# Flamingo gated cross-attention with a mixture of experts: the residual moved from VectorE to ScalarE and GpSimd, its bias to TensorE, prelude and last batch in another order

## The reference

```python
# attention, per batch
q = layernorm(x) @ wq + bq ; k = ctx @ wk + bk ; v = ctx @ wv + bv      # 16 heads
score = (q k^T) / sqrt(16) * mask
score = where(score == 0, -1e9, score)
heads = softmax(score) v  @ wo + bo
x = x + tanh(g_xattn) * heads
# experts, per token
probs = softmax(layernorm(x) @ router_w + router_b); top 2, renormalized -> gates
x = x + tanh(g_ffn) * sum_e gates_e * (silu(xn @ w1_e) * (xn @ w3_e)) @ w2_e
```

## Time and profile before

| | |
|---|---|
| three runs, median (lowest to highest) | 487.54 us (487.33 to 488.08) |
| profiled execution | 488.64 us |
| its span in the trace | 486.7 us |
| PE busy | 460.7 us, 95% |
| PEld busy | 433.4 us, 89% |
| DVE busy | 378.6 us, 78% |
| ACT busy | 307.0 us, 63% |
| POOL busy | 196.0 us, 40% |

### The profile page before, as it was taken

The page is one execution under the profiler, slowest core; times in us unless marked ns, Lnnn a source line. Parts: engine busy times, 40 slices in busy tenths (PEclk is TensorE's granted clock), DMA queues, the critical chain, the costliest instruction groups (busy, mean ns, idle before and its releaser), DMA issues.

```text
span 486.7 us, 11552 instructions
## 1 busy us (share of the span) xinstructions
PE 460.7 (95%) x3720; PEld 433.4 (89%) x3720; DVE 378.6 (78%) x876; ACT 307.0 (63%) x768; POOL 196.0 (40%) x204
## 2 busy tenths in 40 slices
PE   7899899989869999999999999999999999999995
PEld 5578797877767999899999999999999999999894
DVE  1577998978964888886888888888878878878772
ACT  2426555464435667686767767777767767776782
POOL 4428686597784045342146253113303303302312
PEclk9989999999979999999999999999999999999999
DMA  8619998842113104032023132122112102102112
GB/s 256 162 42 392 380 410 312 335 179 90 39 50 112 47 22 90 12 80 24 23 31 70 38 66 45 24 44 26 33 33 44 21 22 33 22 13 34 23 13 23
DMA packets 33968, 45.22 MB, mean 93 GB/s; under 512 B 10183, under 2 KB 30613, under 8 KB 33685
## 3 DMA queue, kind: packets, MB, share of 16 engines
q1 hardware_dynamic: 25999, 35.21, 21.6%
q0 software_dynamic: 6576, 8.92, 10.9%
q10 hardware_dynamic: 1344, 0.48, 0.5%
HBM read 32.91 MB, written 21.82 MB: 112 GB/s over the span
## 4 chain that ended last, share of the span: by engine, by line
PE 68%; DVE 16%; ACT 5%; issue 4%; POOL 3%; ACTq 1%; DMA 1%; DVEq 0%; SPq 0%; POOLq 0%
PE ps_rows L1764 22%; PE ps_wide L1784 7%; PE ps_probT L1764 7%; PE ps_misc L1784 7%; PE ps_wide L1593 5%; DVE w_lo L1404 3%; PE ps_misc L1615 2%; PE ps_misc L1547 2%; PE ps_rows L1813 2%; DVE w_lo L1400 2%; PE ps_probT L1573 2%; PE ps_wide L1824 1%; PE ps_rows L1561 1%; DVE score L1314 1%; DVE ps_rows L1409 1%
## 5 line engine op out<-in xcount | busy, mean ns | idle before, releaser
L1227 POOL DMA_INDIRECT out_x<-y_out,meta x35 | 64.0, 1830 | 190.9 <-ACT y_out L1026 185.8
L1404 DVE TENSOR_TENSOR w_lo<-w,w_hi 128x512 fp32r<-128x512 f32 x152 | 104.1, 685 | 13.4 <-issue 6.6
L1764 PE MATMUL ps_rows<-xt_hi,w_hi 128*128 128x256 f32 x384 | 110.6, 288 | 0.2 <-DVE xt_lo L1418 0.2
L1764 PE MATMUL ps_rows<-xt_hi,w_lo 128*128 128x256 f32 x384 | 108.6, 283 | 0.0
L1764 PE MATMUL ps_rows<-xt_lo,w_hi 128*128 128x256 f32 x384 | 108.6, 283 | 0.0
L975 ACT CAST w_hi<-w 128x512 fp32r x152 | 95.2, 627 | 4.2 <-issue 3.9
L1764 PEld LDWEIGHTS ps_rows<-xt_hi,w_hi 128*128 128x128 f32 x384 | 73.6, 192 | 0.4 <-DVE xt_lo L1418 0.4
L1764 PEld LDWEIGHTS ps_rows<-xt_lo,w_hi 128*128 128x128 f32 x384 | 73.6, 192 | 0.0
L1764 PEld LDWEIGHTS ps_rows<-xt_hi,w_lo 128*128 128x128 f32 x384 | 73.5, 192 | 0.0
L989 ACT ACTIVATE act_g<-ps_rows 128x256 f32<-128x256 f32 x96 | 37.3, 389 | 28.7 <-PE ps_rows L1764 24.0
L1004 ACT CAST hid_hi<-ps_rows 128x256 fp32r<-128x256 f32 x96 | 36.1, 376 | 27.1 <-DVE ps_rows L1409 26.3
(11 more groups left out here) (241 smaller groups left out, 1160.9 us busy)
## 6 DMA issues: line engine op xcount, KB each, us to landing
grouped<-in_pad SPq DMA_DIRECT2D x1, 10296.0 KB
w<-in_L_ffn_w SPq DMA_DIRECT2D x8, 1024.0 KB, 12.2
w2s<-in_L_ffn_w SPq DMA_DIRECT2D x4, 1024.0 KB, 13.7
xg<-grouped SPq DMA_DIRECT2D x16, 256.0 KB, 2.7
out_x<-xall SPq DMA_DIRECT2D x8, 256.0 KB, 7.0
xall<-in_x SPq DMA_DIRECT2D x1, 1024.0 KB, 12.6
xall<-in_x SPq DMA_DIRECT2D x1, 768.0 KB, 7.9
ctxT<-in_ctx_t SPq DMA_DIRECT2D x2, 308.0 KB, 5.4
```

The costliest lines, as they stand in the source:

```text
L1227: pool.indirect_dma_start(out, bass.IndirectOffsetOnAxis(ap=meta[:, s % 2, t, E:E + 1].bitcast(U32), axis=0), y_out[:, s % 2, t, :], None, ...
L1404: dve.tensor_tensor(w_lo[:, f % NB], unit_weights(e, f), w_hi[:, f % NB].bitcast(F32), ALU.subtract).then_inc(w_lo_done, 1)
L1764: mm = pe.matmul(ps_gu[f % NB][:, m, 0:n], lhs, rhs[:, a, c, 0:n], start=(k == 0), stop=(k % (3 * DC) == 3 * DC - 1), skip_group_check=True)
```

## The change

1. **Residual.** For batches 0 to 5 VectorE's fused add goes from `body`. ScalarE's new `gain_copy(b-1)` copies `ps_misc * tanh_g` into a new SBUF buffer `gain` at the end of its body b, and GpSimd's new `add_gain(b-1)` adds that to `xall` at the end of its body b, behind `keys(b+1, 1)`. Batches 6 and 7 keep VectorE's add. `turn_x` and `turn_ctx` now wait for ScalarE's copy (`attended_out`).
2. **Bias.** GpSimd's eight `bias_add` go. `bos` is no longer scaled, and `project_o` begins with a product of one row: ones times `bos`, over both tiles, 512 columns.
3. **Prelude.** The last four strips of `vblock` are issued by GpSimd instead of ScalarE, ahead of its body 0, on a semaphore of their own. ScalarE's `norm(1)` and `xT_copy(1)` move out of body 0 to between its copies of the values. TensorE does `turn_x(1)` and `project_q(1)` earlier; `values(3)` goes to the bank `ps_probT` in place of `ps_misc`.
4. **Last batch.** GpSimd's `context(6, 1)` goes ahead of `deviation2`. VectorE's slot counts of group 0 leave body 6, but for a first one, for steps 1 and 3 of body 7.

The core of the diff:

```diff
-        ps_vals = [ps_probT, ps_route, ps_wide, ps_misc]
+        ps_vals = [ps_probT, ps_route, ps_wide, ps_probT]
...
-                place_values(sp, 0, STRIPS[:-BY_ACT])
-                place_values(sp, 1, STRIPS)
+                place_values(sp, 0, STRIPS[:-BY_POOL], ld_vblock[0])
+                place_values(sp, 1, STRIPS, ld_vblock[1])
...
                 def q_copy(b):
                     act.wait_ge(q_done, b + 1)
+                    if b:
+                        act.wait_ge(scores_done, RG * DC * b)
...
+                def gain_copy(b):
+                    act.wait_ge(wo_done, b + 1)
+                    if b == 0:
+                        act.wait_ge(tanh_done, 1)
+                    else:
+                        act.wait_ge(x2_done, b)
+                    act.activation(gain[:].rearrange("p t d -> p (t d)"), ps_misc[:], ACT.Copy, scale=tanh_g[:, 0:1]).then_inc(attended_out, 1)
...
-                            act.wait_ge(tanh_done, 1)
-                            act.activation(bos, ps_misc[:, 0:D], ACT.Copy, scale=tanh_g[:, 0:1]).then_inc(bo_ready, 1)
+                            act.copy(bos, ps_misc[:, 0:D]).then_inc(bo_ready, 1)
...
                         probT_exp(b, 2, first)
+                    if not first:
+                        gain_copy(b - 1)
...
                 q_copy(0)
+                norm(1)
                 vals_copy(2)
                 vals_copy(3)
-                place_values(act, 0, STRIPS[-BY_ACT:])
+                xT_copy(1)
...
-                def bias_add(b):
-
-                    pool.wait_ge(norm_done, 2 * b + 2)
-                    pool.tensor_tensor(xall[:, bass.ds(b * QT, QT), :], xall[:, bass.ds(b * QT, QT), :], wide(bos, QT),
-                                       ALU.add).then_inc(biased, 1)
+                def add_gain(b):
+
+                    pool.wait_ge(attended_out, b + 1)
+                    pool.tensor_tensor(xall[:, bass.ds(b * QT, QT), :], xall[:, bass.ds(b * QT, QT), :], gain[:], ALU.add).then_inc(x2_done, 1)
...
-                    if b in BEGIN:
+                    if b in BEGIN and not last:
                         deviation2(pool, BEGIN[b])
...
                         context(pool, b - 1, 1)
+                    if last:
+                        deviation2(pool, BEGIN[b])
...
                         keys(b + 1, 1)
-                    if first:
-                        pool.wait_ge(bo_ready, 1)
-                        bias_add(b)
-                        bias_add(b + 1)
+                    if not first and not last:
+                        add_gain(b - 1)
...
                 keys(0, 1)
+                place_values(pool, 0, STRIPS[-BY_POOL:], ld_vblock_end)
...
-                    dve.wait_ge(biased, b + 1)
+                    dve.wait_ge(x2_done, b)
...
                         if s == 0 and b > 1:
-                            residual(b - 2)
                             batch_stats(dve, b - 2)
                         if (b, s) == (B - 2, 0):
+                            hand_out_count(dve, 0)
+                        if (b, s) == (B - 1, 1):
                             hand_out(dve, 0)
-                        if (b, s) == (B - 2, 1):
+                        if (b, s) == (B - 1, 3):
                             hand_out_begin(dve, 0)
                             hand_out_owner(dve, 0)
-                        if (b, s) == (B - 1, 1):
                             hand_out_rest(dve, 0)
...
-                        pe.wait_ge(x2_done, b - 2)
+                        pe.wait_ge(attended_out, b - 2)
...
                     pe.wait_ge(ctxT_copied, b + 1)
+                    pe.matmul(ps_misc[:].rearrange("p (t d) -> p t d", t=QT), one_row[0:1, :], wide(bos[0:1, :], QT),
+                              start=True, stop=False, skip_group_check=True)
...
                 scores(0, 0, True)
+                turn_x(1)
                 values(2)
-                pe.wait_ge(q_copied, 2)
+                project_q(1)
+                pe.wait_ge(vals_copied, 2)
                 values(3)
-                turn_x(1)
                 scores(0, 1, True)
-                project_q(1)
```

More of the change, by code:

```diff
@@ L38 @@
 STRIPS = [(c, h, max(c * P, h * SK), min(c * P + ROWS[c], (h + 1) * SK)) for c in range(NC) for h in range(HEAD0[c], HEAD0[c] + HEADS[c])]
-BY_ACT = 4
+BY_POOL = 4
 NS = 2 * QT
@@ L204, in flamingo_block @@
         ctxnT = sb("ctxnT", [P, DC, SQ])
+        gain = sb("gain", [P, QT, D])
         meta = sb("meta", [P, 2, TH, ROW - D])
@@ L266, in flamingo_block @@
         kblock_done = sem("kblock_done")
+        ld_vblock_end = sem("ld_vblock_end")
         ld_vblock = [sem(f"ld_vblock{i}") for i in range(2)]
         ctxT_done, ctxT_copied = sem("ctxT_done"), sem("ctxT_copied")
-        biased = sem("biased")
+        attended_out = sem("attended_out")
         scores_done, masked, soft_step, lowest_found, lowered = sem("scores_done"), sem("masked"), sem("soft_step"), sem("lowest_found"), sem("lowered")
@@ L339, in norm2 @@
             if k == 0:
-                for landed in ld_vblock:
-                    act.wait_ge(landed, 16 * len(STRIPS))
+                act.wait_ge(ld_vblock_end, 16 * BY_POOL)
+                act.wait_ge(ld_vblock[0], 16 * (len(STRIPS) - BY_POOL))
+                act.wait_ge(ld_vblock[1], 16 * len(STRIPS))
             if k > 1:
@@ L455, in fill @@
             if k == 0:
-                for landed in ld_vblock:
-                    pool.wait_ge(landed, 16 * len(STRIPS))
+                pool.wait_ge(ld_vblock_end, 16 * BY_POOL)
+                pool.wait_ge(ld_vblock[0], 16 * (len(STRIPS) - BY_POOL))
+                pool.wait_ge(ld_vblock[1], 16 * len(STRIPS))
             if k > 1:
@@ L518, in flamingo_block, with hand_out_count @@
         HAND = 20
-        def hand_out(dve, i):
-            at = HAND * i
+        def hand_out_count(dve, i):
             dve.wait_ge(ranked, i + 1)
@@ L525, in hand_out @@
                                      op0=ALU.add, op1=ALU.subtract).then_inc(handed, 1)
+        def hand_out(dve, i):
+            at = HAND * i
             dve.wait_ge(handed, at + 1)
@@ L729, in is_slot, with place_values @@
             return isinstance(s, int) and s == n
-        def place_values(eng, i, some):
+        def place_values(eng, i, some, landing):
             eng.wait_ge(vblock_cleared, 1)
@@ L737, in place_values @@
             for c, h, r0, r1 in some:
-                eng.dma_start(vblock[r0 - c * P:r1 - c * P, c, h - HEAD0[c], mine], vals[r0 - h * SK:r1 - h * SK, h, mine]).then_inc(ld_vblock[i], 16)
+                eng.dma_start(vblock[r0 - c * P:r1 - c * P, c, h - HEAD0[c], mine], vals[r0 - h * SK:r1 - h * SK, h, mine]).then_inc(landing, 16)
         with nc.Block(no_gpsimd_drain=True) as block:
@@ L883, in body @@
                         turned2_copy(act, BEGIN[b - 1], 2)
-                    if not last:
+                    if not last and not first:
                         norm(b + 1)
@@ L1178, in body @@
                         keys(b + 1, 0)
-                    elif not last and not first:
-                        bias_add(b + 1)
                     if b - 1 in FINAL:
@@ L1389, in _ @@
                 context(dve, B - 1, 0)
+                hand_out_count(dve, 1)
                 hand_out(dve, 1)
@@ L1485, in routing @@
                     if u == 8:
+                        hand_out_count(dve, 2)
                         hand_out(dve, 2)
@@ L1530, in turn_x @@
                         pe.wait_ge(q_copied, 2 * b)
-                    if b == 1:
-                        pe.wait_ge(vals_copied, B)
                     if b == 2:
@@ L1588, in attend @@
                         pe.wait_ge(weighed_done, n)
-                    if s == 0 and b % (B // 2) == 0:
-                        pe.wait_ge(ld_vblock[b // (B // 2)], 16 * len(STRIPS))
+                    if s == 0 and b == 0:
+                        pe.wait_ge(ld_vblock_end, 16 * BY_POOL)
+                        pe.wait_ge(ld_vblock[0], 16 * (len(STRIPS) - BY_POOL))
+                    if s == 0 and b == B // 2:
+                        pe.wait_ge(ld_vblock[1], 16 * len(STRIPS))
                     for c in range(NC):
@@ L1599, in turn_ctx @@
                     pe.wait_ge(ctx_done, DC * (b + 1))
-                    if last:
+                    if b == B - 1:
                         pe.wait_ge(x2_done, b)
+                    elif last:
+                        pe.wait_ge(attended_out, b)
                     else:
@@ L1615, in project_o @@
                             mm = pe.matmul(ps_misc[:, t * D:(t + 1) * D], ctxnT[:, g, t * P:(t + 1) * P], wos[:, g, :],
-                                           start=(g == 0), stop=(g == DC - 1))
+                                           start=False, stop=(g == DC - 1), skip_group_check=True)
                     mm.then_inc(wo_done, 1)
```

1 line of the change is left out of this document (removed).

## The result

The changed kernel takes 506.07 us (median of four executions, 500.20 to 512.53) against 487.62: a ratio of 1.0289, 95% interval 1.0246 to 1.0332. That ratio leaves out the two executions over 1.5% above the kernel's own fastest, 509.1 and 512.5 us. In a later comparison (e7) it took 506.51 us (504.24 to 509.09), ratio 1.0412 (1.0372 to 1.0451). The forecast was 496.2 and its range 489.5 to 501.0. The direction was right; the time lies 5 us above the range. The profiled execution, 500.20 us with a span of 498.3, is the shortest of the four; that it lies inside the range is luck.

What follows compares the result with a forecast made beforehand. TensorE and VectorE were taken to share the bound between output projections, with GpSimd joining in one later stretch. Nine terms, from -3.2 to +3.7, summed to +8.7 us: 497.3 profiled, 496.2 beside the median; range 489.5 to 501.

Steps and rivals of the forecast that it cites:

- Clock: +1.0: Projection of batch 6: low TensorE clock behind holes at the old place catches about 1 us; bounds 0 to 3.0.
- the clock falls twice: Rival: half rate behind TensorE's hole before scores (6,0) and again at batch 6's projection; +4, 500.2 us, chance 0.17.
- the bias products: One-row TensorE products at 0.87 us each: +2.6 in batches 1 to 3, +1.7 in 4 and 5, +0.9 in 7.
- TensorE alone: Rival: GpSimd's queue is absorbed, all seven bias products count at 0.87; +2.9, 490.4 us, chance 0.18.
- GpSimd's queue, +3.7: Batch 5: batch 3's add stands ahead of group 0's gates, delaying gates, keys and scores (6,0); bounds 1.3 to 4.4.
- Statistics, +1.3: Copy and add delay VectorE's statistics behind a projection; TensorE waits for them in batch 3; lower end 0.
- VectorE merely waits: Part of the statistics term: outside batch 3 the later statistics only make VectorE wait, at no cost.
- Scatters +0.5: Batch 6: batch 4's add ahead of two GpSimd scatters loses 1.9 us; 1.4 return through the moved slot counts.
- batch 7 +0.2: Up to the projection of batch 6: the reordering in the last batch repays what GpSimd's queue takes, leaving +0.2.
- Prelude, -3.2: Prelude, batches 0 and 1: masked products 1.6 us earlier, 1.6 from freed VectorE and GpSimd; bounds 1.6 to 3.8.
- VectorE's relief: Rival: VectorE loses 0.75 us in each of six batches and the relief reaches the end; -4.2, 483.3 us, chance 0.12.

Runs made afterwards that it cites:

- e7: The changed kernel run again as it is, with a second profile: 506.51 us (504.24 to 509.09), ratio 1.0412 to the kernel before.
- e14: e9 with the bias product of the output projection left out: 491.80 us, ratio 1.0093 to the kernel before.
- e2: The changed kernel with the residual back on VectorE as one fused add, bias still a one-row product: 490.65 us, ratio 1.0062 to the kernel before.
- e3: The kernel before with the new prelude and new last batch only, residual and bias adds as before: 483.67 us, ratio 0.9926.
- e9: The changed kernel with the bias product on 128 rows and products of zeros in TensorE's holes: 496.73 us, ratio 1.0176 to the kernel before.
- e10: The changed kernel with the residual back on VectorE and the bias product on 128 rows: 486.80 us, ratio 0.9984 to the kernel before.
- e13: e9 with GpSimd's residual add cut to 4 of 512 columns, the wait for ScalarE's copy kept: 490.64 us, ratio 1.0072 to the kernel before.
- e1: The changed kernel with GpSimd's add moved behind the first "lower" of the next body: 500.53 us, ratio 1.0296 to the kernel before.
- e4: The kernel before with the new prelude alone: 485.76 us, ratio 0.9963.

## Why the prediction was wrong

| us | forecast | first profile | second profile |
|---|---|---|---|
| up to the projection of batch 0 | -3.2 | -3.53 | -3.66 |
| batches 1 to 3 | +3.9 | +4.31 | +4.31 |
| batch 4 | +4.6 | +4.70 | +8.99 |
| batch 5 | +1.4 | +1.45 | +1.45 |
| batch 6 | +1.2 | +3.41 | +3.24 |
| batch 7 | +0.9 | +1.62 | +1.55 |
| sum | +8.7 | +11.96 | +15.88 |

(From the table of starts, rows rounded. The queue with its bias product is batch 4, the clock term stands in batch 6. The forecast's -3.2 was meant for the prelude with batches 0 and 1.)

- **The step that failed is "Clock: +1.0".** It let one low stretch fall at the old place and bounded it by 3.0 us. By the line through the eight executions, the 14.1 us of missing clock in the middle of the first four cost 11.4 us, against 4.3 for the 5.35 of before: +7 us where the forecast had +1.0 and at most 3.0, and no fixed amount, since it differs from execution to execution. I had tied the fall to holes alone. The one-row product as a second cause was in no term and no rival.
- **The rival "the clock falls twice"** (500.2 us, 0.17) had the hole ahead of scores (6,0) and half rate behind it. The second profile shows just that (112 to 118 us, behind a hole of 2.93 us); the first shows the hole and no fall there. The mechanism was right, its size too small and its chance too low.
- **Without the clock** the kernel lies 11.0 us above before by the same line (494.3 against 487.62 - 4.3 = 483.3), where the sum had 7.7. The split is rough: 59 executions of the kernel before in the later comparisons, the one of 505.52 us left out, have a line of their own, 0.55 us for each us and 484.3 at none, and by it the clock's part is 8.5 us and the rest 10.0. Of the difference to 7.7, the bias products are the larger part. 0.87 is the price with 128 rows (0.85 to 0.87 left out in e14); one row took 1.05 from start to start and cost 1.24 to 1.25 in a stretch (e2 against e3). Of the seven products behind the first projection the sum had six, batch 6's forgotten, though "TensorE alone" counted seven; the one of batch 1 costs nothing in e14. Six at 1.24 less six at 0.87 is 2.2, an estimate, as no run shows the price of one row in batches 6 and 7.
- **GpSimd's queue, +3.7**, the step called decisive, was right: 3.55 for the move in that stretch (e9 against e10), the gates 2.34 us behind the projection, TensorE's hole 2.93 us. Of it the add is 1.0 (e13) and the wait with what stands behind it 2.5, of which the place ahead of the gates makes 2.0 (e1).
- **Statistics, +1.3**: 1.71 (0.76 and 0.95) in batches 1 and 2, where the forecast had "VectorE merely waits", and nothing in batch 3, where it had the cost; so the size was right by luck. The cause was GpSimd's add in the way more than the chain of copy and add as such, since e13 has the chain and not the price.
- **Scatters +0.5, batch 7 +0.2**: the move cost 1.76 and 2.62, the rearranged last batch gave back 0.94 and 1.16 (e3 against e4). That leaves 0.8 and 1.5 without the bias products; the 2.62 hold some clock.
- **Prelude, -3.2**: -3.53, seen alone -3.58. The size is right for a reason that the forecast did not have in full: part of it is clock, since the low stretch of before from 25.0 to 28.5 us is gone. The first attended product came at 26.10, not 27.5.
- **VectorE's relief** did not reach the end: e10, with the adds back on VectorE, is 9.9 us faster than e9.

## What to carry to other kernels

When work goes from a full engine to another, look first at what stands behind it in the new engine's list: an add of 1.27 us that waited 5 us for its input held the gates, the keys and TensorE, and its place cost more than its duration (2.0 against 1.0 us in that stretch). A forecast that rests on half-rate stretches needs a range over where they fall; run the kernel several times and compare the missing clock before believing one profile. Where a bias is added by a product, try it on all 128 rows: here it took no longer than one row (1.02 against 1.12 us), made the stretches 0.38 us shorter at full clock, and the clock no longer fell behind it.

## What was not expected of the hardware

TensorE's clock fell behind a one-row product of 1.12 us with the engine busy 6.63 of the 7 us before; with 128 rows of the same 512 columns it did not. It does not fall behind each such product, but behind 8 of 40. The same program took 500 to 512.5 us, 0.81 us for each us of missing clock. That fits what the Trainium skill says in *TensorE: Matmul & The Clock Gate*, section on the clock gate (the monitor's beat does not start with the kernel, and the same kernel differs from run to run); there it is a matter of the start, here of the middle, and of 2.5% of the time.
